# Rows of the seventh image pair moved as three-row pieces, and the last pair's placing steps set closer together

## The chip, the cores and the metric

The kernel runs on one core of a Trainium2 chip. The metric is the time of one execution on the device in microseconds (us), taken as the median of several executions. Five engines work side by side, each through its own queue in a fixed order: TensorE (PE in the profile), VectorE (DVE), ScalarE (ACT), GpSimd (POOL) and SyncE (SP). POOL's and SP's queues also start the DMA transfers. Engines wait for one another through semaphores that are written out in the kernel.

## The reference

Sixteen images of 128 x 512 become 1024 tokens of 64 channels each. One attention block (softmax over keys along the tokens, softmax of queries over the 8 channels of a head) and one mixture of experts follow, each on a layer-normed input and each with a residual.

```python
def _L0_ffn_ref(x, gate_w, gate_b, w1, w2, w3):
    logits = jnp.einsum('bsd,de->bse', x, gate_w) + gate_b
    probs = jax.nn.softmax(logits, axis=-1)
    top_probs, top_idx = jax.lax.top_k(probs, 2)
    top_probs = top_probs / jnp.sum(top_probs, axis=-1, keepdims=True)
    dispatch = jnp.sum(jax.nn.one_hot(top_idx, n_experts, dtype=x.dtype) * top_probs[..., None], axis=-2)
    h1 = jnp.einsum('bsd,edh->bseh', x, w1)
    h2 = jnp.einsum('bsd,edh->bseh', x, w2)
    hidden = jax.nn.silu(h1) * h2
    expert_out = jnp.einsum('bseh,eho->bseo', hidden, w3)
    return jnp.einsum('bseo,bse->bso', expert_out, dispatch)
h = _L0_tok_ref(x, L0_tok_W, L0_tok_b, L0_tok_pos_embed)
h = h + _L0_attn_ref(_layernorm(h, axis=-1), ...)
h = h + _L0_ffn_ref(_layernorm(h, axis=-1), ...)
```

Only the two chosen experts of a token count, so the kernel computes only these.

## The kernel before

The 16 images go in 8 pairs, counted 0 to 7 here as in the code; the seventh pair is pair 6, the last one pair 7. A pair has 2048 tokens, as 16 columns of 128.

*Front part of a pair.* Embedding, attention, the second layer norm and the gate's logits run in about twenty steps; `Plan` says in which step or half step of a pair each operation stands, `BEGUN` at which step of the program a pair begins (pair 6 at 65, pair 7 at 78). Then every token is placed: `pick` finds its two experts, the rank matmuls count how many rows come before it for the same expert, and `find_places` turns that into row numbers in a table sorted by expert. The table lies in DRAM (`rows_scratch`).

*Moving the rows.* For pairs 0 to 6, POOL scatters the rows to the table by 32 indirect DMAs (line 674): per column one for the first expert, one for the second, 128 rows of 512 bytes each. Pair 7 is in `PIECED`: there a column's 256 rows are first sorted on the chip. VectorE builds a 0/1 matrix, the route (lines 1257 and 1262), TensorE multiplies the rows by it (line 1538, three matmuls a column), ScalarE copies the result out (line 842), and POOL writes it with one indirect DMA of 96 pieces of three rows (line 661), so 16 instead of 32. Tiles of such a pair have 126 rows in place of 128, and it has 13 groups of four tiles where the others have 12.

*Back part.* The table is read back by SP in groups of four tiles, one group per step. In step s TensorE does, in this order: the input products of group g = s - 23 (`project_in`), the transposes of the hidden units of g - 1 (`turn_hidden`, bank `hidT_ps`), the operations of the pairs that stand at s, the transposes of the rows of g + 2 (`turn`, bank `turn_ps`, line 1571), the output products of g - 2 (`project_out`, line 1614), and the operations that stand at s + 0.5. ScalarE copies the banks out and forms tanh, VectorE multiplies. SP stores the outputs to DRAM (`y_scratch`).

*Collecting.* POOL gathers a pair's outputs back to its tokens by 32 indirect DMAs (line 691); `GATHER` names the step at which they begin. `SUMS` names the steps in which ScalarE weighs a quarter of them (line 860) and VectorE adds the second half and the residual (line 1317). Pair 7 is gathered in 16 pieces (line 703) and summed by TensorE through gated routes (lines 1548 and 1562) at the very end.

*What sets the order.* All of this is written out step by step. On POOL the loop over the steps issues, in each step, first the pieces, then the scatters, then the gathers that the tables put there. An engine whose next instruction waits holds all that stands behind it. SP's load of a pair's first group waits until all its scatters have landed, and the stores behind it wait with it.

Of the kernel before, what the change touches and what calls it, by code (L numbers as in the profile page):

```python
# [34 lines left out]
PIECED = (7,)  # L35
# [25 lines left out]
    qturn mixed attend added squares2 ssq2 normed2 zturn zparts logits pick rank odds count base tiles bases2 ends owner""")  # L61
# [3 lines left out]
             rank=15, odds=15, count=15, base=15.5, tiles=None, bases2=None, ends=15.5, owner=16)  # L65
# [3 lines left out]
             rank=16, odds=15.5, count=16.5, base=17, tiles=None, bases2=None, ends=17.5, owner=18)  # L69
# [4 lines left out]
         LATER, LATER, LATER, LATER, LATER._replace(tiles=17.5, bases2=18, ends=18.5, owner=19))  # L74
# [72 lines left out]
def vit_kernel(nc, x, tok_w, tok_b, pos, wk, bk, wq, bq, wv, bv, wr, br, gate_w, gate_b, w1, w2, w3, out):  # L147
# [4 lines left out]
    with ExitStack() as ctx:  # L152
# [6 lines left out]
        def sem(name):  # L159
# [129 lines left out]
        piece_at = sb("piece_at", [P, COLS], U32)  # L289
# [20 lines left out]
                x_cols0[:, :, :].rearrange("p j c -> p (j c)"), squares[:, :])  # L310
        pieces = [place[:, n * one:(n + 1) * one] for place, count in zip(flat, (10, 2, 2, 2)) for n in range(count)]
        assert len(pieces) == COLS and one == PIECE * P
# [47 lines left out]
        pieces_out = sem("pieces_out")  # L360
# [24 lines left out]
        def routes_at(half):  # L385

            for m in PIECED:
                for j in range(COLS):
                    if ROUTES[m] + j // 2 == half:
                        yield m, j  # L390
# [152 lines left out]
        def _(pool):  # L543
# [178 lines left out]
            for s in range(SPAN):  # L722
# [7 lines left out]
                for m, j in gathers_at(s):  # L730
                    if m in PIECED:
# [5 lines left out]
        def _(act):  # L737
# [97 lines left out]
            def take_piece(m, j):  # L835
                wait(act, "piece_ps_ready", j + 1)
                if j == 0:
                    wait(act, "emb_ps_ready", 2 * PAIRS)
                    wait(act, "mean_ps_ready", PAIRS)
                    wait(act, "x_turned", PAIRS)  # L840
                    wait(act, "logits_ps_ready", PAIRS)
                sc.activation(pieces[j][0:PIECES, :], piece_place(j)[0:PIECES, 0:PIECE * 2 * E], ACT.Copy).then_inc(S["piece_ready"], 1)

            def take_gates(j):
# [3 lines left out]
                sc.activation(pieces[j][0:PIECES, :], piece_place(j)[0:PIECES, 0:PIECE * P], ACT.Copy).then_inc(S["gates_turned"], 1)  # L848
# [21 lines left out]
            for s in range(SPAN):  # L870
# [13 lines left out]
                for m, j in routes_at(2 * s - 1):  # L884
                    take_piece(m, j)
# [7 lines left out]
                for m, q in sums_at(s):  # L893
                    if m not in PIECED:
# [3 lines left out]
        def _(dve):  # L898
# [117 lines left out]
            def attend(m, k):  # L1016
# [184 lines left out]

            def find_places(m):
# [466 lines left out]
```

## Time and profile before

| | us |
|---|---|
| median of 3 runs | 754.61 |
| the three runs | 757.6, 754.61, 754.32 |
| profiled execution | 757.5 |
| its span, first to last instruction | 755.7 |
| PE busy | 622.1 (82%) |
| DVE busy | 476.6 (63%) |
| ACT busy | 353.2 (47%) |
| POOL busy | 503.5 (67%) |
| mean granted TensorE clock | 0.877 of full speed |

The span is what the trace covers; 1.8 us of the execution lie around it. Busy shares are means over stages with different limits, so the rows below are taken stage by stage. POOL's busy time counts an indirect DMA from when it is taken up to when its descriptors are written; the pause of 0.30 us before the next one is not counted. "L674" is line 674 of the kernel before.

### The profile page before, as it was taken

What the parts mean: (1) busy time and instruction counts of PE and PEld (TensorE: products, weight loads), DVE (VectorE), ACT (ScalarE), POOL (GpSimd) and SP (SyncE); (2) the same over time, 40 slices, a digit from 0 to 9 for tenths busy, and PEclk for the clock granted to TensorE, in tenths of its full rate; (3) what the DMA queues carried; (4) which work ended last, traced back from release to release, by engine and by line L of the source; (5) the groups of instructions that cost most, each with busy time, mean ns of one, the idle gap of its engine ahead of it and who ended that gap; (6) DMA issues with size and microseconds to landing.
All of it is one profiled execution on the core that took longest, in us unless ns stands there. A gap on an engine that the chain in (4) does not pass through costs nothing.

```text
span 755.7 us, 13960 instructions
## 1 busy us (share of the span) xinstructions
PE 622.1 (82%) x4059; PEld 519.8 (69%) x4059; DVE 476.6 (63%) x1322; ACT 353.2 (47%) x774; POOL 503.5 (67%) x537
## 2 busy tenths in 40 slices
PE   5886687788979998999889998998894888799328
PEld 3365454666568967886779687967884787798228
DVE  5654645567556677767666756766585687598410
ACT  2121311226355647564656456545562557486400
POOL 4362044757577477777777777777777777777773
PEclk9958778589989999999999989998998789898755
DMA  3499504134184329542844284537351635664322
GB/s 82 90 175 345 203 29 111 49 108 120 56 226 132 95 55 230 136 131 65 208 134 131 62 204 120 135 82 165 92 149 57 164 98 158 175 150 98 68 59 59
DMA packets 169200, 94.52 MB, mean 125 GB/s; under 512 B 99551, under 2 KB 153207, under 8 KB 169129
## 3 DMA queue, kind: packets, MB, share of 16 engines
q1 hardware_dynamic: 152728, 67.65, 34.5%
q0 software_dynamic: 15616, 25.59, 12.8%
q8 instruction: 38, 0.62, 0.4%
q10 hardware_dynamic: 784, 0.39, 0.2%
q14 instruction: 34, 0.27, 0.1%
HBM read 45.40 MB, written 48.18 MB: 124 GB/s over the span
## 4 chain that ended last, share of the span: by engine, by line
PE 51%; DVE 20%; issue 9%; POOL 7%; DMA 6%; ACT 5%; ACTq 0%; SPq 0%; POOLq 0%; DVEq 0%
PE h_ps L1593 8%; PE wide_ps L1381 7%; PE y_ps L1614 5%; PE hidT_ps L1606 4%; PE turn_ps L1571 3%; PE wide_ps L1401 3%; DMA hx<-xi_scratch 2%; PE wide_ps L1504 2%; DVE twice_y L1298 2%; POOL rows_scratch L674 2%; POOL kexp L691 2%; POOL hx L691 2%; DMA xi_scratch<-xi 2%; PE wide_ps L1387 2%; ACT sums L860 2%
## 5 line engine op out<-in xcount | busy, mean ns | idle before, releaser
L674 POOL DMA_INDIRECT rows_scratch<-z_parts,place x224 | 224.5, 1002 | 126.9 <-issue 64.9
L691 POOL DMA_INDIRECT sums<-y_scratch,place x192 | 185.1, 964 | 66.2 <-issue 56.4
L1593 PE MATMUL h_ps<-w_hi,rowsT 128*128 (+1 forms) x388 | 117.8, 330 | 15.8 <-DVE hid_all L1300 15.4
L1298 DVE SCALAR_TENSOR_TENSOR twice_y<-tanh,h_ps 128x256 f32<-128x256 f32 (+1 forms) x194 | 80.4, 414 | 52.5 <-ACT tanh L818 31.2
L1593 PE MATMUL h_ps<-w_lo,rowsT 128*128 (+1 forms) x388 | 105.6, 298 | 0.0
L1614 PE MATMUL y_ps<-w_sb,hidT_all 128*128 (+1 forms) x776 | 103.1, 279 | 1.4 <-ACT twice_y L833 1.4
L1614 PEld LDWEIGHTS y_ps<-w_sb,hidT_all 128*128 128x128 f32 (+1 forms) x776 | 100.2, 202 | 2.3 <-issue 2.3
L1593 PEld LDWEIGHTS h_ps<-w_hi,rowsT 128*128 128x128 f32 (+1 forms) x388 | 78.8, 203 | 25.9 <-issue 22.3
L818 ACT ACTIVATE tanh<-h_ps 128x256 f32<-128x256 f32 (+1 forms) x194 | 69.6, 386 | 46.5 <-PE h_ps L1593 42.6
L1300 DVE SCALAR_TENSOR_TENSOR hid_all<-twice_y,h_ps 128x256 f32<-128x256 f32 (+1 forms) x194 | 81.6, 421 | 6.7
L1571 PE MATMUL turn_ps<-ident,rows_all 128*128 128x128 f32 (+1 forms) x388 | 64.4, 292 | 21.0 <-DMA rows_all<-rows_scratch 14.2
L1593 PEld LDWEIGHTS h_ps<-w_lo,rowsT 128*128 128x128 f32 (+1 forms) x388 | 79.7, 206 | 0.3
L807 ACT ACTIVATE rowsT<-turn_ps 128x512 fp32r<-128x512 f32 (+1 forms) x97 | 57.7, 594 | 32.4 <-PE turn_ps L1571 32.0
L1606 PE MATMUL hidT_ps<-ident,hid_all 128*128 128x128 f32 (+1 forms) x388 | 66.2, 299 | 6.7 <-issue 3.6
L1571 PEld LDWEIGHTS turn_ps<-ident,rows_all 128*128 128x128 f32 (+1 forms) x388 | 47.9, 150 | 34.3 <-issue 18.4
L827 ACT ACTIVATE hidT_all<-hidT_ps 128x512 f32<-128x512 f32 (+1 forms) x97 | 58.6, 604 | 16.3 <-PE hidT_ps L1606 14.7
L1381 PE MATMUL wide_ps<-w_patch,x_cols 64*128 64x512 f32 x224 | 56.4, 634 | 3.2 <-DVE w_patch L917 3.2
L1606 PEld LDWEIGHTS hidT_ps<-ident,hid_all 128*128 128x128 f32 (+1 forms) x388 | 48.5, 153 | 11.8 <-issue 9.9
L833 ACT ACTIVATE twice_y<-y_ps 128x256 f32<-128x256 f32 (+1 forms) x97 | 37.1, 382 | 30.0 <-DMA y_scratch<-twice_y 20.2
L1381 PEld LDWEIGHTS wide_ps<-w_patch,x_cols 64*128 64x128 f32 x224 | 21.4, 197 | 23.4 <-issue 18.9
L776 ACT ACTIVATE vals<-wide_ps 128x256 f32<-128x256 f32 x28 | 10.7, 383 | 55.3 <-DVE qs L1055 55.3
L1317 DVE SCALAR_TENSOR_TENSOR sums<-sums,gate 128x64 f32<-128x64 f32 x96 | 21.0, 280 | 21.9 <-ACT sums L860 21.9
(350 smaller groups left out, 1107.0 us busy)
## 6 DMA issues: line engine op xcount, KB each, us to landing
rows_all<-rows_scratch SPq DMA_DIRECT2D x84, 256.0 KB
y_scratch<-twice_y SPq DMA_DIRECT2D x84, 128.0 KB
rows_scratch<-tanh SPq DMA_DIRECT2D x3, 3276.0 KB
xi_scratch<-xi SPq DMA_DIRECT2D x16, 256.0 KB
hx<-xi_scratch SPq DMA_DIRECT2D x14, 256.0 KB
rows_scratch<-z_parts,place POOLq DMA_INDIRECT x224
out<-sums SPq DMA_DIRECT2D x56, 64.0 KB
x_in<-in_x SPq DMA_DIRECT2D x26, 128.0 KB
```

Of the source, the lines that this page charges most:

```text
L674: gp.indirect_dma_start(rows_dram[n], bass.IndirectOffsetOnAxis(ap=place[m % RING][:, r, j:j + 1], axis=0), z_parts[m % 2][:, j // 2, j % ...
L691: gp.indirect_dma_start(y_of[r][apart(m)][:, j // 2, j % 2, :], None, y_dram[m % 3][0:GROUPS[m] * GROUP * width(m), :], bass.IndirectOffse ...
L807: sc.activation(rowsT[g % 2][:, 0:GROUP * w], turn_ps[:, 0:GROUP * w], ACT.Copy).then_inc(S["rowsT_ready"], 1)
L818: sc.activation(tanh[0:w, j, :], h_ps[0:w, :].rearrange("p (j n h) -> p j n h", j=GROUP, n=2)[:, j, 0, :], ACT.Tanh, scale=0.5).then_inc(S ...
L827: sc.activation(hidT[g % 2][:, 0:GROUP * w], hidT_ps[:, 0:GROUP * w], ACT.Copy).then_inc(S["hidT_ready"], 1)
L1298: ve.scalar_tensor_tensor(twice[0:w, j, :], tanh[0:w, j, :], 1.0, halves[:, j, 0, :], ALU.add, ALU.mult).then_inc(S["twice_done"], 1)
L1300: ve.scalar_tensor_tensor(hid[g % 2][0:w, j, :], twice[0:w, j, :], 0.5, halves[:, j, 1, :], ALU.mult, ALU.mult).then_inc(S["hid_done"], 1)
L1381: te.matmul(wide_ps[:, b * 512:(b + 1) * 512], x_cols[second(m)][half, j, :], w_patch[half, j, :, :].rearrange("p t e -> p (t e)"), start= ...
L1571: mm = te.transpose(turn_ps[:, j * w:(j + 1) * w], rows[g % 3][0:w, j, :, :].rearrange("p n e -> p (n e)"), ident[0:w, 0:w])
L1593: mm = te.matmul(h_ps[0:w, j * 256:(j + 1) * 256], rowsT[g % 2][:, j * w:(j + 1) * w], w12[:, bass.ds(experts[g][j], 1), :, :].rearrange(" ...
L1606: mm = te.transpose(hidT_ps[:, j * w:(j + 1) * w], hid[g % 2][0:w, j, :], ident[0:w, 0:w])
L1614: mm = te.matmul(y_ps[0:w, j * E:(j + 1) * E], hidT[g % 2][:, j * w:(j + 1) * w], w3_sb[:, bass.ds(e, 1), :].rearrange("h a d -> h (a d)") ...
```

## The change

Pair 6 joins pair 7 in `PIECED`: its rows go as pieces. While pair 7's pieces use the front part's own bank `wide_ps`, which is free by then, pair 6's front part shares the chip with pair 7's, so its pieces take turns in the two banks of the tiles: an even column in `turn_ps`, an odd one in `hidT_ps` (`piece_place`). The waits that keep these uses apart are added to `move_rows`, `turn` and `turn_hidden`; ScalarE's copy of a piece moves ahead of its copy of the hidden units. `ROUTES` gets a start in half steps and a number of columns for each half step: one column for pair 6 from half step 169, two for pair 7 from 191 (196 before). The finding of the moves is a function of its own with a place in the plan. Pair 7's placing operations stand half a step to two and a half steps earlier, its mean and means one and a half and two steps later. The gathers of pair 4 begin at step 86 (91 before), those of pair 5 at 98 (102), of pair 7 at 124 (123), and the sums are shifted with them. Pair 6 has 13 groups, so there are 98 groups in place of 97.

```diff
-PIECED = (7,)
+PIECED = (6, 7)
...
 PLANS = (AT_ONCE._replace(mean=3.5), AT_ONCE._replace(mean=2.5), FIRST,
-         LATER, LATER, LATER, LATER, LATER._replace(tiles=17.5, bases2=18, ends=18.5, owner=19))
+         LATER, LATER, LATER, LATER._replace(tiles=17.5, bases2=18.75, moves=19, ends=19.5, owner=20),
+         LATER._replace(mean=8, means=8.5, rank=15.5, count=15.5, base=16, tiles=16, bases2=16.5, moves=16.5, ends=17, owner=17.5))
...
-ROUTES = (None, None, None, None, None, None, None, 196)
-
-GATES = 105
+ROUTES = {6: (169, 1), 7: (191, 2)}
+
+GATES = 104
...
-SCATTER = (16, 22, 28, 44, 59, 72, 85, None)
-GATHER = (38, 51, 65, 78, 91, 102, 111, 123)
-SUMS = ([[43 + 14 * m + q for q in range(4)] for m in range(5)]
-        + [[112, 113, 114, 115], [121, 122, 122, 123], [124, 125, 126, 127]])
+SCATTER = (16, 22, 28, 44, 59, 72, None, None)
+GATHER = (38, 51, 65, 78, 86, 98, 111, 124)
+SUMS = ([[43 + 14 * m + q for q in range(4)] for m in range(4)]
+        + [[94, 95, 96, 97], [107, 108, 109, 110], [122, 123, 123, 124], [125, 126, 127, 128]])
...
-        def piece_place(j):
-
-            return wide_ps[:, j % 2 * 512:(j % 2 + 1) * 512]
+        def in_between(m):
+
+            return m < PAIRS - 1
+
+        def piece_place(m, j):
+
+            return (turn_ps, hidT_ps)[j % 2][:, :] if in_between(m) else wide_ps[:, j % 2 * 512:(j % 2 + 1) * 512]
...
                 if 0 <= g < GROUPS_ALL:
                     activate(g)
+                for m, j in routes_at(2 * s - 1):
+                    take_piece(m, j)
                 if 0 <= g - 1 < GROUPS_ALL:
                     copy_hidT(g - 1)
                 if 0 <= s - GATES - 2 < COLS:
                     take_gates(s - GATES - 2)
-                for m, j in routes_at(2 * s - 1):
-                    take_piece(m, j)
...
+            def find_moves(m):
+
+                i = nth(m)
+                wait(dve, "base_ps_ready", m + 1)
...
-            def move_rows(m, j):
-
+            def move_rows(m, j, g):
+
+                i = COLS * nth(m) + j
                 if j == 0:
                     wait(pe, "z_split", m + 1)
-                    wait(pe, "piece_at_ready", 1)
-                wait(pe, "route_ready", j + 1)
-                wait(pe, "piece_ready", j - 1)
+                    wait(pe, "piece_at_ready", nth(m) + 1)
+                if in_between(m):
+
+                    wait(pe, *(("rowsT_ready", g + 2), ("hidT_ready", g))[j % 2])
+                wait(pe, "route_ready", i + 1)
+                wait(pe, "piece_ready", i - 1)
...
                 wait(pe, "rowsT_ready", g)
+                wait_pieces(2 * (g - 2 + LAG) - 1)
...
                 wait(pe, "hidT_ready", g)
+                wait_pieces(2 * (g + LAG))
+                if g + LAG == step_of(PIECED[0], 18):
+                    wait(pe, "moves_ready", 2)
...
                 if 0 <= g < GROUPS_ALL:
                     project_in(g)
+                for m, j in routes_at(2 * s - 1):
+                    move_rows(m, j, g)
                 if 0 <= g - 1 < GROUPS_ALL:
                     turn_hidden(g - 1)
                 for m, k in steps_at(s):
                     attend(m, k)
-                for m, j in routes_at(2 * s - 1):
-                    move_rows(m, j)
```

POOL's queue from the end of pair 3's gathers on. Before, one pair's launches stand together: pair 6's scatters, pair 4's gathers, pair 7's pieces, pair 5's gathers.

```order
L674 DMA rows_scratch<-z_parts,place 6552x128 x32
L691 DMA sums<-y_scratch,place 128x64 x32
L661 DMA rows_scratch<-w_patch,piece_at 3744x384 x10
L661 DMA rows_scratch<-x_in,piece_at 3744x384 x2
L661 DMA rows_scratch<-x_cols,piece_at 3744x384 x2
L661 DMA rows_scratch<-squares,piece_at 3744x384 x2
L691 DMA sums<-y_scratch,place 128x64 x32
```

Now, from the same place (L667 are pieces, L697 gathers; pair 6's pieces end with the two from `base`, pair 7's begin with the ten from `w_patch`):

```order
L667 DMA rows_scratch<-w_patch,piece_at 3744x384 x4
L697 DMA sums<-y_scratch,place 128x64 x4
L667 DMA rows_scratch<-w_patch,piece_at 3744x384 x2
...
L667 DMA rows_scratch<-base,piece_at 3744x384 x2
L697 DMA sums<-y_scratch,place 128x64 x4
L667 DMA rows_scratch<-w_patch,piece_at 3744x384 x10
L667 DMA rows_scratch<-x_in,piece_at 3744x384 x2
L697 DMA sums<-y_scratch,place 128x64 x4
L667 DMA rows_scratch<-x_cols,piece_at 3744x384 x2
L667 DMA rows_scratch<-squares,piece_at 3744x384 x2
L697 DMA sums<-y_scratch,place 128x64 x28
```

Pair 6's 16 pieces have 28 of pair 4's gathers between them, in runs of 4, 4, 6, 4, 6 and 4, and the remaining 4 behind; 4 of pair 5's gathers stand among pair 7's pieces.

TensorE in step 86, from the input products on to the transposes of the next rows; before (the third query of pair 7 is L1398 and L1401):

```order
L1577 TENSOR_LOAD owner [waits owner_ready]
L1606 MATMUL hidT_ps<-ident,hid_all 128x128 [waits hidT_ready,hid_done]
L1606 MATMUL hidT_ps<-ident,hid_all 128x128 x3
L1398 MATMUL wide_ps<-qv_bias,ones_r 128x512 [waits q_shifted,v_ready]
L1401 MATMUL wide_ps<-proj_qv,hx 128x256 x2
L1571 MATMUL turn_ps<-ident,rows_all 128x128 [waits rowsT_ready,rows_in2]
L1571 MATMUL turn_ps<-ident,rows_all 128x128 x3
```

The same place now (L1570 is a piece of pair 6, L1523 pair 7's mean):

```order
L1616 TENSOR_LOAD owner [waits owner_ready]
L1570 MATMUL turn_ps<-z_parts,route 96x128 [waits piece_ready,route_ready,rowsT_ready]
L1570 MATMUL turn_ps<-z_parts,route 96x128 x2
L1648 MATMUL hidT_ps<-ident,hid_all 128x128 [waits piece_ready,hidT_ready,hid_done]
L1648 MATMUL hidT_ps<-ident,hid_all 128x128 x3
L1422 MATMUL wide_ps<-qv_bias,ones_r 128x512 [waits q_shifted,v_ready]
L1425 MATMUL wide_ps<-proj_qv,hx 128x256 x2
L1523 MATMUL side_ps<-w_mean,x_cols 128x16 [waits owner_ready]
L1523 MATMUL side_ps<-w_mean,x_cols 128x16 x7
L1610 MATMUL turn_ps<-ident,rows_all 128x128 [waits piece_ready,rowsT_ready,rows_in2]
L1610 MATMUL turn_ps<-ident,rows_all 128x128 x3
```

The wait for `rowsT_ready`, which stood behind the hidden units and the query, now stands ahead of them, and the turn also waits for the copy of the piece.

TensorE around the turn of pair 6's first group, now (L1610 is that turn, L1538 the count of pair 7's rows, which before stood one step later):

```order
L1610 MATMUL turn_ps<-ident,rows_all 128x126 [waits rowsT_ready,rows_in0]
L1610 MATMUL turn_ps<-ident,rows_all 128x126 x3
L1656 ISA [waits y_ready,hidT_ready]
...
L1538 MATMUL side_ps<-ones_b,hot_b 128x1 [waits hot_ready]
L1538 MATMUL side_ps<-ones_b,hot_b 128x1
```

The count has moved up to half a step behind the turn, and not ahead of it.

## Rows read from the trace of the kernel before

**Rows 1.** The page: busy tenths in 40 slices of the span, POOL.

```profile
POOL 4362044757577477777777777777777777777773
```

**Rows 2.** Windows of POOL: start:end, us, busy us (count), PE clock, DMA share, GB/s.

```profile
540.35:582.77 42.42, 32.67 (x32) 0.93 0.38 103
623.15:643.43 20.28, 15.40 (x17) 0.92 0.58 160
685.24:725.52 40.28, 30.52 (x32) 0.76 0.33 70
```

**Rows 3.** Timelines of POOL and PE: start, us, what [idle before <-releaser].

```profile
581.51 0.96 POOL L674 DMA_INDIRECT rows_scratch<-z_parts,place  x1 [0.30 <-issue]
586.54 1.11 PE L1571 MATMUL turn_ps<-ident,rows_all 128*128 128x128 f32 x4 [10.49 <-DMA rows_all<-rows_scratch]
```

**Rows 4.** Timelines of POOL and PE, pair 7's last piece and first group.

```profile
642.21 0.91 POOL L661 DMA_INDIRECT rows_scratch<-squares,piece_at  x1 [0.30 <-issue]
647.87 0.67 PE L1571 MATMUL turn_ps<-ident,rows_all 126*128 126x126 f32 x4 [3.76 <-DMA rows_all<-rows_scratch]
```

**Rows 5.** Timelines of PE, ACT and DVE around step 86.

```profile
529.59 1.91 PE L1495 MATMUL side_ps<-w_mean,x_cols 128*128 128x16 f32 x16
537.29 0.60 PE L1606 MATMUL hidT_ps<-ident,hid_all 128*128 128x128 f32 x4
539.79 0.63 PE L1571 MATMUL turn_ps<-ident,rows_all 128*128 128x128 f32 x4 [0.80 <-ACT rowsT L807]
...
539.07 0.58 ACT L807 ACTIVATE rowsT<-turn_ps 128x512 fp32r<-128x512 f32 x1
544.00 1.05 ACT L779 ACTIVATE qs<-qs 128x1024 f32<-128x1024 f32 x1
...
539.20 0.87 DVE L1317 SCALAR_TENSOR_TENSOR sums<-sums,gate 128x64 f32<-128x64 f32 x4 [1.77 <-ACT sums L860]
```

**Rows 6.** Pair 7's placing: timelines of PE and DVE, and a group of the page.

```profile
588.06 1.97 PE L1614 MATMUL y_ps<-w_sb,hidT_all 128*128 x8 [0.41 <-ACT twice_y L833]
595.98 0.20 PE L1464 MATMUL side_ps<-counted_all,same_expert_b 128*16 128x1 bf16 x2
...
593.09 0.15 DVE L1167 TENSOR_SCALAR thirds<-side_ps 128x2 f32<-128x2 f32 x1
593.79 0.53 DVE L1175 TENSOR_SCALAR counted_all<-ones,counted 128x128 bf16<-128x128 f32 x2
597.76 0.29 DVE L1193 TENSOR_SCALAR tiles_all<-ones,tiles 16x128 bf16<-16x128 f32 x1
601.14 0.75 DVE L1211 TENSOR_TENSOR placed<-hot,side_ps 128x256 f32<-128x256 f32 x2
605.24 0.16 DVE L1223 TENSOR_SCALAR place<-slots_u 128x32 uint32<-128x32 uint32 x1
...
L1300 DVE SCALAR_TENSOR_TENSOR hid_all<-twice_y,h_ps 128x256 f32<-128x256 f32 (+1 forms) x194 | 81.6, 421 | 6.7
```

**Rows 7.** Timelines of PE, DVE and ACT: pair 7's pieces, the first and last two.

```profile
611.19 0.71 PE L1538 MATMUL wide_ps<-z_parts,route 128*96 128x128 f32 x6
...
632.87 1.26 PE L1538 MATMUL wide_ps<-z_parts,route 128*96 128x128 f32 x6
...
622.00 0.65 DVE L1257 TENSOR_SCALAR route<-slot_id,slots_f 128x288 fp32r<-128x288 f32 x2
622.56 0.94 DVE L1262 SCALAR_TENSOR_TENSOR route<-slot_id,slots_f,route 128x288 fp32r<-128x288 f32 x2
...
623.63 0.92 ACT L842 ACTIVATE w_patch<-wide_ps 96x384 f32<-96x384 f32 x2 [2.00 <-PE wide_ps L1538]
```

**Rows 8.** Timelines of PE and ACT: output products, and pair 5's last quarter weighed.

```profile
657.74 1.00 PE L1614 MATMUL y_ps<-w_sb,hidT_all 128*128 x8
672.59 0.99 PE L1614 MATMUL y_ps<-w_sb,hidT_all 128*126 x8
704.82 1.09 PE L1614 MATMUL y_ps<-w_sb,hidT_all 128*126 x8 [0.39 <-ACT twice_y L833]
...
686.85 1.44 ACT L860 ACTIVATE sums<-sums,mean_all,gate 128x64 f32<-128x64 f32 x4 [1.15 <-DMA sums<-y_scratch,place]
```

More of the change, by code:

```diff
@@ L60 @@
 Plan = namedtuple("Plan", """embed squares normed bases mean means keys kmax kexp kturn queries values qexp qsum context scales mix
-    qturn mixed attend added squares2 ssq2 normed2 zturn zparts logits pick rank odds count base tiles bases2 ends owner""")
+    qturn mixed attend added squares2 ssq2 normed2 zturn zparts logits pick rank odds count base tiles bases2 moves ends owner""")
 FIRST = Plan(embed=(0.75, 1, 1.5, 2), squares=2.5, normed=2.5, bases=3.5, mean=5.5, means=5.5, keys=4.5, kmax=4.5, kexp=5, kturn=5,
@@ L64 @@
              attend=10, added=10.5, squares2=10.5, ssq2=11, normed2=11.5, zturn=12.5, zparts=12.5, logits=13, pick=13.5,
-             rank=15, odds=15, count=15, base=15.5, tiles=None, bases2=None, ends=15.5, owner=16)
+             rank=15, odds=15, count=15, base=15.5, tiles=None, bases2=None, moves=None, ends=15.5, owner=16)
 LATER = Plan(embed=(1, 1.5, 2, 2), squares=2.5, normed=2.5, bases=3.5, mean=6.5, means=6.5, keys=5, kmax=5.5, kexp=6, kturn=6,
@@ L68 @@
              attend=11, added=11.5, squares2=11.5, ssq2=12, normed2=12.5, zturn=13.5, zparts=13.5, logits=14, pick=14.5,
[L69 removed]
+             rank=16, odds=15.5, count=16.5, base=17, tiles=None, bases2=None, moves=None, ends=17.5, owner=18)
 AT_ONCE = FIRST._replace(zturn=12, logits=12.5, pick=12.5, rank=13, count=13, odds=14.5, base=13.5, ends=13.5, owner=14)
 PLANS = (AT_ONCE._replace(mean=3.5), AT_ONCE._replace(mean=2.5), FIRST,
[L74 removed]
+         LATER, LATER, LATER, LATER._replace(tiles=17.5, bases2=18.75, moves=19, ends=19.5, owner=20),
+         LATER._replace(mean=8, means=8.5, rank=15.5, count=15.5, base=16, tiles=16, bases2=16.5, moves=16.5, ends=17, owner=17.5))
 XI_OUT, HX_IN, X_NEXT = 2, 3, 4
@@ L288, in vit_kernel @@
         moves = placed[0]
-        piece_at = sb("piece_at", [P, COLS], U32)
+        piece_at = [sb(f"piece_at{n}", [P, COLS], U32) for n in range(2)]
         piece_from = sb("piece_from", [P, COLS], U32)
@@ L309, in vit_kernel @@
         flat = (w_patch[:, :, :, :].rearrange("p j t e -> p (j t e)"), x_in0[:, :, :].rearrange("p r f -> p (r f)"),
-                x_cols0[:, :, :].rearrange("p j c -> p (j c)"), squares[:, :])
-        pieces = [place[:, n * one:(n + 1) * one] for place, count in zip(flat, (10, 2, 2, 2)) for n in range(count)]
-        assert len(pieces) == COLS and one == PIECE * P
+                x_cols0[:, :, :].rearrange("p j c -> p (j c)"))
+        pieces = [[place[:, n * one:(n + 1) * one] for place, count in zip(flat + (last,), (10, 2, 2, 2)) for n in range(count)]
+                  for last in (base0[:, :, :, :].rearrange("p t b e -> p (t b e)"), squares[:, :])]
+        assert len(pieces[0]) == COLS and one == PIECE * P
         x_in = (x_in0[:, :, :], twice_y[:, :].rearrange("p (r f) -> p r f", r=2))
@@ L359, in vit_kernel @@
         scattered = [sem(f"scattered{n}") for n in range(3)]
-        pieces_out = sem("pieces_out")
+        pieces_out = [sem(f"pieces_out{n}") for n in range(len(PIECED))]
         rows_in = [sem(f"rows_in{n}") for n in range(3)]
@@ L1112, in attend @@
                     count_tiles(m)
+                if k == plan.moves:
+                    find_moves(m)
                 if k == plan.ends:
```

95 lines of the change are left out of this document (57 added, 38 removed).

## The prediction

> **What bounds the kernel now.** I read the slices of the page first: POOL's row stands at 7 in every slice from the fifteenth, about 265 us, to the last but one [rows 1]. That is no engine with a quarter of its time free. The windows of three stretches of POOL show 32 launches in 42.42 us, 16 in 20.28 and 32 in 40.28 [rows 2]: one indirect DMA each 1.26 to 1.33 us, of which about 0.95 is counted busy, with the next one close behind. (The x17 counts a neighbour at the edge.) So from about 265 us POOL is a queue that never empties, and the order of the launches in it is fixed. The end is POOL too: after the last gathers of pair 6 at 725.52 come the 16 of pair 7 and the closing sums, 755.7 - 725.52 = 30.2 us.
>
> Then I read where TensorE waits for this queue. The scatter of pair 6 ends late: its last launch starts at 581.51 and TensorE, idle for 10.49 us, turns the pair's first tile group at 586.54 [rows 3]. For pair 7, which already goes as pieces, the last launch starts at 642.21 and its first group is turned at 647.87, 5.66 us later [rows 4]. Taking launches out of the queue before 581 therefore looks like pure gain. The question is whether POOL still has something to launch.
>
> **The change, part by part.** I follow three hinges: T, the turn of pair 6's first group (586.54 before); X, the end of POOL's gathers of pair 5 (685.24); and the end (755.7).
>
> *POOL's saving.* 32 scatters of rows (42.42 us) become 16 of pieces (20.28 us): 22.1 us less in the queue [rows 2]. One piece costs 20.28/16 = 1.27 us, one gather 40.28/32 = 1.26.
>
> *Its new order, up to T.* Before, all 32 scatters stood together. Now 28 of the 32 gathers of pair 4 stand between the pieces (first order fence). POOL is free for pair 6 at 540.35 as before, since nothing ahead of it changes. The sixteenth piece starts at 540.35 + 15 x 1.27 + 28 x 1.26 = 594.7, if POOL never waits; with the 5.66 us of rows 4, T = 600.3. So the interleaving alone makes T 13.8 us later, though POOL has then done most of pair 4's gathers, which before came after 582.77.
>
> *What the pieces add in TensorE's steps.* Four pieces stand at the head of that queue without a gather between them, so the fourth is wanted at 540.35 + 3 x 1.27 = 544.2. It comes at the end of the step in which pair 7's third and fourth queries are formed. ScalarE can copy it only behind the exponential of the queries, which before ran from 544.00 to 545.05 [rows 5]; with half of 0.92 for the copy [rows 7] that is 545.5, a wait of 1.3 us at the least, and T = 601.6. The step also grows. The piece in the turn bank needs the copy out of that bank, the one TensorE waited for until 539.79; the transposes and the query, which ran before that wait (537.29 to 539.79 less the wait of 0.80, 1.70 us), now stand behind it (second order fence), and so does pair 7's mean, moved there from a step and a half earlier (1.91 us). To this come the product (half of 0.90), two pieces' routes on VectorE (622.00 to 623.50, 1.50) and two copies (0.92) [rows 5, 7]. Together 6.5 us: the fourth piece at 552.0, a wait of 7.8, T = 608.1. VectorE's own gap of 1.77 us at 539.20 [rows 5] can hold the routes, so I take T = 608.1 - 1.8 = 606.3, and keep 601.6 and 608.1 for the range. The other pieces come in time: after each pair stand four or six gathers, 5 to 7.6 us, about a step. Routes, copies and products of the later steps lie beside these gathers; without that cover each step would add some 3 us.
>
> *A rule on VectorE beside POOL.* The 16 piece launches of pair 7 took 1.27 us each with route operations running beside many of them, no more than gathers at 1.26 [rows 2, 7], so I add nothing for the 32 new route operations. The Trainium skill ("SBUF — State Buffer", "Who interferes with whom") says that a VectorE copy or tensor-scalar in a two-port mode locks GpSimd out for the whole instruction. By that rule the 16 first route operations of 0.33 us would delay as many launches, 5.3 us, and the time would be 765.2; the 1.27 of the trace includes such operations already and speaks against it, and I leave it 3 chances in 100 inside the slowest case below.
>
> *The last pair's small operations.* They move up by up to five half steps: count, base, tiles, moves and places now follow within two steps. But its count matmuls stand behind the turn at T in TensorE's order, so none runs during the stall; the chain starts there. From T: the output products end at 588.06 + 1.97 - 586.54 = 3.5; count 1.2 (593.09 to 594.32); base and tiles 2.1 (595.98 to 598.05); one tile multiply of four operations at 0.42, 1.7; moves and places 4.3 (601.14 to 605.40); one sum of pair 4 on VectorE 1.3 (0.87 and a longer 0.42, estimate); another multiply 1.7; routes 1.5; product and copy 0.9 [rows 5 to 7]. That is 18.2, and six hand-overs between engines at an estimate of 0.2 (539.07 + 0.58 to 539.79 shows 0.14) make 19.4. Before, the first two pieces were ready after 611.19 - 586.54 = 24.7 on TensorE, but POOL was not there until 623.15.
>
> *From T to X.* Two pieces follow every (632.87 - 611.19)/7 = 3.10 us [rows 7], so pieces eleven and twelve are ready at T + 19.4 + 5 x 3.10 = T + 34.9. Behind them POOL has these two, 4 gathers, 4 pieces and 28 gathers: 6 x 1.27 + 32 x 1.26 = 47.9. X = T + 82.8 = 689.1, 3.9 us later than before. POOL meanwhile idles: after the last piece of pair 6 (at T - 4.7, its launch over) only four gathers are left, until T + 0.3; the first piece of pair 7 comes at T + 19.4. These 19 us, with the waits before T, eat the 22.1.
>
> *From X to the end.* POOL gathers pair 6 until X + 40.3. TensorE is held too: ScalarE weighs the last quarter of pair 5 in step 110 (115 before) and stands there until the gather lands. Before, it began that at 686.85, X + 1.6, and the last output product came 17.97 us and six steps later, at 704.82. Now twelve steps follow, six more at (672.59 - 657.74)/5 = 2.97 [rows 8]; the thirteenth tile group of pair 6 is one of them. Product at X + 1.6 + 18.0 + 17.8 = X + 37.4; its 1.1, the copy and the store to DRAM are an estimate of 4.3, half of rows 4's two DMAs and 1.5 for the rest. So pair 7's outputs lie there at X + 41.7 and POOL waits 1.4 us. End: X + 41.7 + 30.2 = X + 71.9 = 761.0.
>
> *At nothing:* the removed rank matmuls of pair 6, its count and moves (they lie in steps in which POOL is behind anyway); pair 7's old stall of 3.76 us [rows 4], which goes, since its pieces now end some six steps ahead of their turn, but TensorE then waits in step 110 instead; the longer descriptors, in the 1.27.
>
> *Sum.* 761.0 against the span of 755.7: +5.3. The profiled execution took 757.5 in all, so it would take 762.8. The median of the three runs is 754.61, below the profiled one; the difference put on it gives 759.9 us, and the rivals below stand on the median too.
>
> **Rivals.** *The queue stays full:* if pair 7's pieces are ready when pair 4's gathers end, all 22.1 us come back: 732.5. For it: rows 2. Against it: the chain of 19.4 us behind T has only 5 us of gathers as cover. *A shorter chain:* T at its low end (-4.7), the sum and one multiply beside TensorE's work (-3.0), hand-overs free (-1.2), no wait at the end (-1.4), 10.3 in all: 749.6. The gap of 1.77 speaks for it; that each step names the other engine's last result, against. *No change:* only T at its low end, 755.2. For it: TensorE and ScalarE also idle in places within those steps; against it: the second order fence, which puts a chain of waits where there was slack. *TensorE becomes the bound of pair 6's pieces:* the shared banks chain TensorE to ScalarE's copies, and each of the eight steps costs 1.50 + 0.92 + 0.45 = 2.9 more, and once the 3.6 of rows 5. TensorE reached the stalled turn at 586.54 - 10.49 = 576.05; it would get there at 602.9, the last piece launched there, T = 608.6 and the time 762.2; were pair 7's pieces, on the same chain, paced at an estimate of 4.0 instead of 3.10, it would be 5 x 0.9 more, 766.7. It decides from about 25 us of added work on (from 576.05 to the 600.9 at which the last launch stands at T = 606.3); below that POOL's queue hides it.
>
> **How the numbers follow.** This measurement can tell 0.5% from no change, 3.8 us: faster is under 750.8, slower over 758.4. Forecast 0.39 (own range 756 to 764, a quarter of it under 758.4), no change 0.27, shorter chain 0.14, full queue 0.08, TensorE as bound 0.12. Faster 0.14 + 0.08 = 0.22; same 0.27 + 0.10 = 0.37; slower 0.29 + 0.12 = 0.41. The range leaves out the full queue and the far end of the last case: 747 to 767.
>
> **What would show it.** Right: the pieces of pair 6 on POOL with a gap of 1 to 8 us before the fourth; the stalled turn near 606; about 20 us in which POOL launches nothing, from then on; no stall before pair 7's first group; ScalarE waiting in step 110 for a gather. Wrong: POOL without a gap from 540 to the end, or a turn before 598, or pair 7's first piece within 14 us of it.

## The result, and the profile after

The changed kernel takes 765.89 us (median of four, 762.46 to 774.62), the kernel before 754.54 beside it. The ratios in this document leave out runs in a slower state, here the 774.62, and compare the means of the others: 764.75 to 755.25, ratio 1.0126, 95% interval 1.0079 to 1.0172. A second series ("changed again" in the table of experiments) gave 767.65 against 755.38, 1.0148 (1.0098 to 1.0197). So the change costs 9.5 to 11.2 us. Forecast were 759.9 and a range of 747 to 767; the second median lies just outside it.

| profiled execution | before | after |
|---|---|---|
| execution, span | 757.5, 755.7 | 765.45, 763.7 |
| PE, DVE, ACT busy | 622.1, 476.6, 353.2 | 633.5, 490.9, 362.5 |
| POOL busy | 503.5 | 489.5 |

The page's slices of the changed kernel show where POOL runs dry; before, every digit from the fifteenth to the last but one was 7 [rows 1]:

```profile
POOL 4353047767574777777777777777377616777773
```

The 3 that breaks the long run of 7s is the slice from 534.6 to 553.7 us, the 6 and the 1 that follow it the slices from 592 to 630. POOL's windows from its first launch for pair 6 (P from here on) to the first gather of pair 7, before and then after (us, busy us with the count of instructions, PE clock, DMA share, GB/s):

```profile
540.35:725.52 185.17, 141.26 (x144) 0.85 0.48 120
```

```profile
533.99:733.46 199.47, 125.58 (x128) 0.86 0.45 115
```

Sixteen launches fewer, 14.3 us more. POOL's timeline after (start, us, instruction, idle before and its releaser) has the reason: pair 6's first four pieces, its last piece and the last of the four gathers behind it, pair 7's first piece:

```profile
533.99 0.94 POOL L667 DMA_INDIRECT rows_scratch<-w_patch,piece_at  x1 [0.30 <-PE turn_ps L1610]
538.50 0.93 POOL L667 DMA_INDIRECT rows_scratch<-w_patch,piece_at  x1 [3.57 <-ACT w_patch L853]
541.97 0.91 POOL L667 DMA_INDIRECT rows_scratch<-w_patch,piece_at  x1 [2.54 <-ACT w_patch L853]
549.21 0.91 POOL L667 DMA_INDIRECT rows_scratch<-w_patch,piece_at  x1 [6.33 <-ACT w_patch L853]
...
601.17 0.93 POOL L667 DMA_INDIRECT rows_scratch<-base,piece_at  x1 [0.30 <-issue]
...
606.19 0.94 POOL L697 DMA_INDIRECT sums<-y_scratch,place  x1 [0.30 <-issue]
626.28 0.93 POOL L667 DMA_INDIRECT rows_scratch<-w_patch,piece_at  x1 [19.15 <-ACT w_patch L853]
629.61 0.91 POOL L667 DMA_INDIRECT rows_scratch<-w_patch,piece_at  x1 [1.16 <-ACT w_patch L853]
...
692.55 0.94 POOL L697 DMA_INDIRECT hx<-y_scratch,place  x1 [0.30 <-issue]
...
733.46 0.93 POOL L709 DMA_INDIRECT sums<-y_scratch,piece_from  x1 [0.30 <-issue]
```

A pause of 0.30 belongs to every launch. What goes beyond it adds up to 11.54 us ahead of the second, third and fourth pieces, 18.85 ahead of pair 7's first and 4.52 among pair 7's pieces (the 1.16 is the first of five): 34.91. The rest, 199.47 - 34.91 = 164.56, is 1.286 us for each of 128 launches, and 185.17/144 is 1.286 too. So the change saved 20.6 us of launches and lost 34.9 in waits.

The turn T that pair 6's first group waits for, and the chain behind it to pair 7's first piece (timelines of PE, DVE and ACT; [rows 3, 6, 7] are the same operations before):

```profile
606.46 1.10 PE L1610 MATMUL turn_ps<-ident,rows_all 126*128 126x126 f32 x4 [9.38 <-DMA rows_all<-rows_scratch]
609.45 0.24 PE L1538 MATMUL side_ps<-ones_b,hot_b 128*128 128x1 bf16 x2
612.39 0.20 PE L1488 MATMUL side_ps<-counted_all,same_expert_b 128*16 128x1 bf16 x2
614.93 0.59 PE L1504 MATMUL wide_ps<-to_piece,counted_all 128*96 128x512 bf16 x2
624.26 1.15 PE L1570 MATMUL wide_ps<-z_parts,route 128*96 128x128 f32 x6
...
617.35 0.86 DVE L1341 SCALAR_TENSOR_TENSOR sums<-sums,gate 128x64 f32<-128x64 f32 x4
622.86 0.64 DVE L1281 TENSOR_SCALAR route<-slot_id,slots_f 128x288 fp32r<-128x288 f32 x2
...
693.62 1.43 ACT L871 ACTIVATE sums<-sums,mean_all,gate 128x64 f32<-128x64 f32 x4 [6.43 <-DMA sums<-y_scratch,place]
```

The count (609.45) stands behind the turn, the tile work and one sum of pair 4 (617.35) stand between, and the first product comes at T + 17.8. The last row is ScalarE's wait in step 110.

The two traces don't begin alike. TensorE's windows of 110 to 165 us, long before the change acts, before and after:

```profile
110.00:165.00 55.00, 42.68 (x197) 0.75 0.30 85
```

```profile
110.00:165.00 55.00, 41.88 (x231) 0.81 0.33 95
```

The profiled execution of before was granted a lower clock in this stretch and reached P 6.4 us later (540.35 against 533.99). This stretch alone does not settle P: "thinner again" below had 0.75 in it too, and its P was 534.17. But over the fourteen profiles P goes with the mean granted clock of the first 265 us: 533.99 to 534.88 in the five with 0.88, 539.16 to 540.35 in the three with 0.85 (one of them with pieces for pair 6). So the experiments are compared by distances from P, and the times by their ratios.

### The profile page after: what moved, and what is told of

Its sections match the earlier page's. It is cut to its first block, busy times and chain, and to the rows that moved or that the text cites. A ratio compares the mean times of both kernels' runs of the same rounds, so it can differ in the third digit from the quotient of the medians.

```text
span 763.7 us, 14233 instructions
## 1 busy us (share of the span) xinstructions
PE 633.5 (83%) x4126; PEld 529.6 (69%) x4126; DVE 490.9 (64%) x1369; ACT 362.5 (47%) x795; POOL 489.5 (64%) x521
## 3 DMA queue, kind: packets, MB, share of 16 engines
q1 hardware_dynamic: 153524, 67.96, 34.9%
## 4 chain that ended last, share of the span: by engine, by line
PE 51%; DVE 20%; issue 10%; POOL 8%; ACT 5%; DMA 5%; ACTq 0%; DVEq 0%; POOLq 0%
PE h_ps L1632 8%; PE wide_ps L1405 7%; PE y_ps L1656 6%; POOL sums L697 5%; PE hidT_ps L1648 4%; PE turn_ps L1610 3%; PE wide_ps L1425 3%; PE wide_ps L1532 2%; DVE twice_y L1322 2%; DMA hx<-xi_scratch 2%; PE wide_ps L1411 2%; POOL rows_scratch L667 2%; DMA xi_scratch<-xi 1%; ACT sums L871 1%; PE h_ps L1600 1%
## 5 line engine op out<-in xcount | busy, mean ns | idle before, releaser
L680 POOL DMA_INDIRECT rows_scratch<-z_parts,place x192 | 192.0, 1000 | 107.8 <-issue 56.4
L697 POOL DMA_INDIRECT sums<-y_scratch,place x192 | 186.9, 973 | 66.2 <-issue 55.8
L1656 PE MATMUL y_ps<-w_sb,hidT_all 128*128 (+1 forms) x784 | 106.8, 283 | 0.8 <-ACT twice_y L839 0.7
L1656 PEld LDWEIGHTS y_ps<-w_sb,hidT_all 128*128 128x128 f32 (+1 forms) x784 | 104.1, 207 | 1.4 <-issue 1.4
L1610 PE MATMUL turn_ps<-ident,rows_all 128*128 128x128 f32 (+1 forms) x392 | 65.7, 294 | 20.7 <-ACT rowsT L813 11.0
L1610 PEld LDWEIGHTS turn_ps<-ident,rows_all 128*128 128x128 f32 (+1 forms) x392 | 49.5, 153 | 34.2 <-issue 23.7
L813 ACT ACTIVATE rowsT<-turn_ps 128x512 fp32r<-128x512 f32 (+1 forms) x98 | 57.9, 591 | 26.3 <-PE turn_ps L1610 26.3
L1648 PEld LDWEIGHTS hidT_ps<-ident,hid_all 128*128 128x128 f32 (+1 forms) x392 | 48.9, 154 | 12.6 <-issue 11.7
L667 POOL DMA_INDIRECT rows_scratch<-w_patch,piece_at x20 | 19.5, 976 | 40.8 <-ACT w_patch L853 37.1
L871 ACT ACTIVATE sums<-sums,mean_all,gate 128x64 f32<-128x64 f32 x96 | 34.2, 430 | 9.1 <-DMA sums<-y_scratch,place 9.1
```

The lines of the kernel that those rows point to most:

```text
L680: gp.indirect_dma_start(rows_dram[n], bass.IndirectOffsetOnAxis(ap=place[m % RING][:, r, j:j + 1], axis=0), z_parts[m % 2][:, j // 2, j % ...
L697: gp.indirect_dma_start(y_of[r][apart(m)][:, j // 2, j % 2, :], None, y_dram[m % 3][0:GROUPS[m] * GROUP * width(m), :], bass.IndirectOffse ...
L813: sc.activation(rowsT[g % 2][:, 0:GROUP * w], turn_ps[:, 0:GROUP * w], ACT.Copy).then_inc(S["rowsT_ready"], 1)
L1610: mm = te.transpose(turn_ps[:, j * w:(j + 1) * w], rows[g % 3][0:w, j, :, :].rearrange("p n e -> p (n e)"), ident[0:w, 0:w])
L1648: mm = te.transpose(hidT_ps[:, j * w:(j + 1) * w], hid[g % 2][0:w, j, :], ident[0:w, 0:w])
L1656: mm = te.matmul(y_ps[0:w, j * E:(j + 1) * E], hidT[g % 2][:, j * w:(j + 1) * w], w3_sb[:, bass.ds(e, 1), :].rearrange("h a d -> h (a d)") ...
```

## The experiments

The theory is the forecast's: POOL's queue sets T, and the placing chain behind T sets pair 7's first piece. The rival: TensorE's and ScalarE's longer steps set both. All distances in us; "pauses" is POOL's idle time beyond 0.30 a launch from P to pair 7's gathers. Distances come from one profile a kernel, and T - P differed by 0.4 us between two profiles of the changed kernel and by 3.3 between two of the thinner one.

| kernel | T - P | first piece - T | pauses | end - P | ratio to before (95%) |
|---|---|---|---|---|---|
| before | 46.2 | 36.6 | 0 | 215.4 | |
| changed | 72.5 | 19.8 | 34.9 | 229.7 | 1.0126 (1.0079 to 1.0172) |
| changed again | 72.8 | 19.7 | 34.9 | 229.1 | 1.0148 (1.0098 to 1.0197) |
| gathers later | 71.4 | 19.3 | 33.1 | 228.2 | 1.0151 (1.0094 to 1.0208) |
| thinner | 71.8 | 20.0 | 35.7 | 229.7 | 1.0120 (1.0084 to 1.0156) |
| thinner again | 68.5 | 19.2 | 31.8 | 225.0 | one run, 760.95 us |
| pieces alone | 74.2 | 19.1 | 57.9 | 251.2 | one run, 790.66 us |
| weighing moved | 68.5 | 19.9 | 31.0 | 225.0 | 1.0120 (1.0053 to 1.0188) |
| placing earlier | 71.6 | 17.0 | 33.5 | 227.4 | 1.0176 (1.0115 to 1.0237) |
| old placing | 73.4 | 28.1 | 46.3 | 241.4 | 1.0318 (1.0242 to 1.0394) |
| placing alone | 46.3 | 26.6 | 0 | 215.9 | 1.0017 (0.9987 to 1.0046) |
| weighing moved, before | 45.5 | 36.6 | 0 | 214.4 | 0.9986 (0.9966 to 1.0006) |
| combined | 60.7 | 16.3 | 20.0 | 215.0 | 1.0000 (0.9965 to 1.0036) |
| combined, sums later | 60.3 | 16.3 | 17.4 | 212.1 | 0.9935 (0.9907 to 0.9964) |

One sum covers the whole table: end - P less the pauses is 193.2 to 195.1 in every kernel with pieces for pair 6, and 214.4 to 215.9 where it goes as rows. The time from P is POOL's launches, its pauses and the closing 30 us. The sum doesn't say what makes the pauses; that is what the edits below are for.

**The gathers begun one step later.**

```diff
-GATHER = (38, 51, 65, 78, 86, 98, 111, 124)
+GATHER = (38, 51, 65, 78, 87, 98, 111, 124)
```

> Changed kernel with the gathers of pair 4 begun one step later (87 for 86), so that 24 instead of 28 of them stand ahead of pair 6's last piece. Theory (GpSimd's queue sets T, the turn of pair 6's first group): the last piece's product was at 593.88 and its launch only at 601.17; with 4 to 6 launches fewer ahead of it, it goes at about 595.5 to 596, T = 600.7 to 601.5 instead of 606.46, pair 7's first piece about 20 us later at 621, the span about 758.5, ratio to before 1.006. Rival (TensorE's lengthened steps set T): T stays at 606, span 764, ratio 1.0126.

T came 1.1 us earlier behind P, not 5 to 6. POOL's first six launches for pair 6 show why:

```profile
540.25 1.20 POOL L667 DMA_INDIRECT rows_scratch<-w_patch,piece_at  x1 [0.31 <-issue]
541.75 0.93 POOL L667 DMA_INDIRECT rows_scratch<-w_patch,piece_at  x1 [0.30 <-issue]
544.14 0.91 POOL L667 DMA_INDIRECT rows_scratch<-w_patch,piece_at  x1 [1.47 <-ACT w_patch L853]
553.02 0.91 POOL L667 DMA_INDIRECT rows_scratch<-w_patch,piece_at  x1 [7.97 <-ACT w_patch L853]
556.50 0.91 POOL L667 DMA_INDIRECT rows_scratch<-w_patch,piece_at  x1 [2.57 <-ACT w_patch L853]
560.31 1.77 POOL L667 DMA_INDIRECT rows_scratch<-w_patch,piece_at  x1 [2.90 <-ACT w_patch L853]
```

The four gathers that left had been cover: pieces five and six now wait 2.57 and 2.90, about as long as four launches take. The theory's size fell, since I took gathers out where the pieces weren't ready; the rival was not shown by it.

**The gathers thinned out late, not early**, and once more for a second profile:

```diff
-    if GATHER[m] + (... (COLS + j * GROUPS_NEXT) // (2 * COLS)) == s:
+    if ((86, 87, 88, 89, 90, 91, 92, 93)[j // 2] if m == 4 else GATHER[m] + (...)) == s:
```

> Changed kernel with 4 launches of pair 4's gathers in each step from 86 to 93 (before 4 or 6), so that 24 and not 28 stand ahead of pair 6's last piece, the first ones where they stood. Distances from the first piece launch of pair 6 (533.99 in the changed kernel), since the traces begin up to 6 us apart. Theory (behind the fourth piece GpSimd's queue sets T): T falls by four launches, 5.0, from 72.5 to 67.5 us after the first piece; pair 7's first piece 5 us earlier with it, span about 759, ratio 1.006. Rival (TensorE's and ScalarE's steps set T): T stays at 72.5, ratio 1.0126.

> The kernel with thinner gathers once more, for a second profile. In the first one TensorE's granted clock was 0.68 from 534 to 550 us (0.96 in the changed kernel's), and the fourth piece came 4.7 us later beside the first. Theory (queue and TensorE's steps bind T together, the clock decides which): with a clock above 0.9 in these windows T is 67 to 69 us behind the first launch. Rival (the thinner gathers do nothing): 72.

The first profile missed (71.8), the second met the expectation (68.5, at a granted clock of 1.00 from 534 to 550). In the first, TensorE was granted the lower level (1.2 of 2.4 GHz) for 541 to 547, where the changed kernel had full clock. TensorE's windows, first profile and changed kernel:

```profile
535.00:541.00 6.00, 3.67 (x20) 0.82 0.29 75
541.00:547.00 6.00, 6.00 (x28) 0.50 0.21 60
```

```profile
535.00:541.00 6.00, 3.67 (x26) 0.97 0.28 88
541.00:547.00 6.00, 6.00 (x48) 1.00 0.33 90
```

It was busy 3.67 of the 6 us ahead of it in both, so these rows do not say why it fell in one. It cost the fourth piece a wait of 11.02 for 6.33. That is the 4.7 us of the expectation; the piece itself came 2.2 us later behind P (17.5 for 15.2), since the second piece had come sooner. In the second profile pair 6's last two pieces and T read:

```profile
593.44 0.93 POOL L667 DMA_INDIRECT rows_scratch<-base,piece_at  x1 [0.30 <-issue]
596.78 1.14 POOL L667 DMA_INDIRECT rows_scratch<-base,piece_at  x1 [2.41 <-ACT base L853]
...
602.71 1.10 PE L1610 MATMUL turn_ps<-ident,rows_all 126*128 126x126 f32 x4 [4.06 <-DMA rows_all<-rows_scratch]
```

Now the last piece waits for its copy. Four launches fewer, and TensorE's and ScalarE's pace sets T. In the time (1.0120) the gain is too small to tell.

**The pieces alone**, all gathers of pair 4 behind them:

```diff
-GATHER = (38, 51, 65, 78, 86, 98, 111, 124)
+GATHER = (38, 51, 65, 78, 93, 98, 111, 124)
...
-        + [[94, 95, 96, 97], ...
+        + [[97, 98, 99, 100], ...
```

> Changed kernel with all gathers of pair 4 put behind pair 6's last piece (begun at step 93; sums of pair 4 at 97 to 100). GpSimd then launches pair 6's pieces as they come. Theory: T falls to what TensorE's and ScalarE's steps allow, last product at 593.88 in the changed kernel, so about 66 us after the first piece launch instead of 72.5, and the launches show waits of several us between most pieces; the 28 gathers come later, so the span is about 15 us longer, near 780. Rival (TensorE's steps already set T in the changed kernel): T stays at 72 or more behind the first piece.

POOL waits before 15 of the 16 pieces, 49 us in all, and T is 74.2 behind P: later than in the changed kernel. The theory's 66 failed, and the rival's sign came true. But the granted clock was 0.71 from 534 to 550 (0.96 in the changed kernel), so this is TensorE's and ScalarE's pace at a low clock. In the changed kernel POOL launched without a pause from the fourth piece to the last, whose product was there at 593.88, 7.3 us ahead of its launch; there the queue set that part of T. My estimate from these runs and thinner again: at a good clock the steps of TensorE and ScalarE allow about 68, at a bad one 74, and POOL's queue, its first waits included, wants 72.5. So the two lie close together; no run has the pieces alone at a full clock.

**ScalarE's weighing moved.** The changed kernel's third piece waited on a chain of ScalarE (timelines of ACT and PE): the weighing of pair 3's sums stands ahead of the copy out of the turn bank, and the piece goes into that bank.

```profile
538.11 1.42 ACT L871 ACTIVATE sums<-sums,mean_all,gate 128x64 f32<-128x64 f32 x4
539.44 0.58 ACT L813 ACTIVATE rowsT<-turn_ps 128x512 fp32r<-128x512 f32 x1
...
540.07 0.47 PE L1570 MATMUL turn_ps<-z_parts,route 128*96 128x128 f32 x3 [2.33 <-ACT rowsT L813]
```

```diff
                 if 0 <= g - 1 < GROUPS_ALL:
                     copy_hidT(g - 1)
+                for m, q in sums_at(s):
+                    if m == 3:
+                        weigh(m, q)
...
-                    if m < PAIRS - 1:
+                    if m < PAIRS - 1 and m != 3:
                         weigh(m, q)
```

> Changed kernel with one edit: ScalarE weighs pair 3's quarters (steps 85 to 88, 1.42 us each) behind its copy of the hidden units, no longer at the end of the step, where the copy out of the turn bank and with it the next piece wait behind it. All 28 gathers stay between the pieces. Theory as forecast (GpSimd's queue sets T): the first four pieces come some 3 us earlier, two steps of 1.4, and T with them, about 69 to 70 us behind the first launch instead of 72.5. Rival (TensorE and ScalarE set T): all four steps count, T falls by 5.7, to 67 behind the first launch. If pieces and queue bind together, the fall is that of the slower of the two, 3 or less, and the span near 761, ratio 1.008.

```profile
534.88 0.94 POOL L667 DMA_INDIRECT rows_scratch<-w_patch,piece_at  x1 [0.30 <-issue]
536.26 0.96 POOL L667 DMA_INDIRECT rows_scratch<-w_patch,piece_at  x1 [0.44 <-ACT w_patch L853]
538.45 0.90 POOL L667 DMA_INDIRECT rows_scratch<-w_patch,piece_at  x1 [1.23 <-ACT w_patch L853]
545.65 0.91 POOL L667 DMA_INDIRECT rows_scratch<-w_patch,piece_at  x1 [6.30 <-ACT w_patch L853]
...
603.38 1.10 PE L1613 MATMUL turn_ps<-ident,rows_all 126*128 126x126 f32 x4 [12.44 <-DMA rows_all<-rows_scratch]
```

T is 68.5 behind P, 4.0 less, between the two expectations, but not all of this is the weighing. It made the third piece's wait 1.23 for 2.54, which was 2.54 or 2.55 in seven of the eight other profiles with pieces for pair 6 and the weighing in its old place. The larger part, 3.57 to 0.44 before the second piece, is not shown to be the edit's: that piece's copy stands ahead of the weighing in the changed kernel, and its wait lay between 0.30 and 3.58 in those eight. TensorE reached the stalled turn 7.0 us sooner behind P (603.38 - 12.44 - 534.88 = 56.1, before 606.46 - 9.38 - 533.99 = 63.1), but its stall grew from 9.38 to 12.44: here POOL's queue sets T. So the weighing cost 1.3 us at the third piece, and this is a cost of the pieces' place in the turn bank that the forecast did not have. In the time (1.0120) nothing can be told from it. The same edit in the kernel before:

> Kernel before with the same edit on ScalarE (pair 3's quarters weighed behind the copy of the hidden units). Theory: pair 6 goes as rows there, GpSimd's queue is full, and nothing of it waits for ScalarE's copy; time as before, ratio 0.997 to 1.003. Rival (the place of the weighing costs by itself): 2 to 5 us faster, ratio 0.994 to 0.997.

0.9986: no gain there, as the theory had it.

**The placing of pair 7**: half a step earlier still, back at the places of before, and moved without the pieces of pair 6.

```diff
-LATER._replace(mean=8, means=8.5, rank=15.5, count=15.5, base=16, tiles=16, bases2=16.5, moves=16.5, ends=17, owner=17.5))
+LATER._replace(mean=8, means=8.5, rank=15, count=15, base=15.5, tiles=15.5, bases2=16, moves=16, ends=16.5, owner=17))
...
-ROUTES = {6: (169, 1), 7: (191, 2)}
+ROUTES = {6: (169, 1), 7: (189, 2)}
```

> Changed kernel with all placing operations of pair 7 half a step earlier still (rank and count at 15, ahead of the stalled turn; base and tiles 15.5, bases2 and moves 16, ends 16.5, owner 17, routes from half step 189). Theory (POOL's 19 us without a launch are the placing chain of pair 7 that starts at T): the count is done during the stall, the chain from T shrinks from 19.8 to about 16 us, T stays at 606.5, the span falls by about 4 to 760, ratio 1.008. Rival (the backlog of tile work after the stall on TensorE and VectorE sets the first piece, not the chain): the first piece stays at T + 19 to 20, span 764, ratio 1.0126.

The count ran in the stall (matmul at 596.29, T at 605.64), and the first piece came at T + 17.0 instead of 19.8. The mechanism held, with 2.8 of the 3.8 us expected. The time did not fall (1.0176): it scatters too widely to show 2.8 us, and 2.3 more were lost among the pieces.

```diff
-LATER._replace(mean=8, means=8.5, rank=15.5, ..., owner=17.5))
+LATER._replace(mean=8, means=8.5, tiles=17.5, bases2=18, moves=18.5, ends=18.5, owner=19))
...
-ROUTES = {6: (169, 1), 7: (191, 2)}
+ROUTES = {6: (169, 1), 7: (196, 2)}
...
-GATES = 104
+GATES = 105
```

> Changed kernel with pair 7's placing operations back at the places of before (rank 16 to owner 19, routes from half step 196); its mean and means stay where the change put them. Theory: GpSimd is free after T but the first piece comes at T + 24.7 or later (the distance of before), 5 to 9 us later than in the changed kernel; span 769 to 773, ratio 1.019 to 1.025. Rival (the places in the plan do not matter, the tile work does): span 764, ratio 1.0126.

```profile
635.74 0.93 POOL L667 DMA_INDIRECT rows_scratch<-w_patch,piece_at  x1 [27.75 <-ACT w_patch L853]
```

The first piece comes at T + 28.1, the pauses grow by 11.4 and end - P by 11.7. So beside pair 6's pieces the closer placing is worth 11.7 us, more than the 5 to 9 expected; without it the change would have cost over 3%.

> Kernel before with only the closer placing operations of pair 7 (and its routes from half step 191, its mean later); pair 6 still goes as rows. Theory: GpSimd has scatters and gathers to launch until about 623 whatever the placing does, so the pieces are ready early and wait for it; time as before, ratio 0.997 to 1.003, the stall of 3.8 us before pair 7's first group remains. Rival (closer operations cost by themselves, on TensorE and VectorE): 3 to 5 us slower, ratio 1.004 to 1.007.

With pair 6 as rows it is worth nothing (1.0017): POOL launches without a pause. Only the stall before pair 7's first group, which the theory had left as it was, fell from 3.76 to 1.21 [rows 4], off POOL's path.

**Combined**, four edits: gathers of pair 4 in fours at steps 85 to 90, 92 and 93, the weighing moved, the placing earlier, sums of pair 5 later; then also the sums of pair 4 out of the chain and the gathers of pair 5 from step 99 (97 in the first). The tables of the second, against the changed kernel:

```diff
-GATHER = (38, 51, 65, 78, 86, 98, 111, 124)
+GATHER = (38, 51, 65, 78, 86, 99, 111, 124)
-        + [[94, 95, 96, 97], [107, 108, 109, 110], ...
+        + [[98, 99, 100, 101], [111, 112, 113, 114], ...
```

> Changed kernel with four edits: gathers of pair 4 in fours at steps 85 to 90, 92 and 93; placing of pair 7 half a step earlier, as in the run with the placing earlier (and gathers of pair 5 from 97); ScalarE weighs pair 3's quarters behind the copy of the hidden units and not at the end of the step, ahead of the copy out of the turn bank; sums of pair 5 at steps 111 to 114. Theory: pieces of pair 6 come 1.4 us earlier in each of four steps, T is 60 to 63 us behind the first piece, the first piece of pair 7 17 us behind T, span 748 to 752, ratio 0.99 to 0.997. Rival (TensorE's steps set T): T at 66 or later, span 755, ratio 1.000 to 1.003.

> As the combined kernel, but the sums of pair 4 at steps 98 to 101 instead of 94 to 97 and the gathers of pair 5 from 99, so that neither ScalarE's weighing (1.43 us a step) nor VectorE's sum (1.3) stands in the placing chain of pair 7. Theory: first piece of pair 7 about 14 us behind T instead of 17, span 745 to 750, ratio 0.985 to 0.993. Rival (these operations lie beside the chain): first piece at T + 17, as the combined kernel.

The first met its distances (60.7 and 16.3), but its ratio was 1.0000, as the rival had it. The pauses fall to 20.0 and 17.4, less than the 20.6 saved, and the second is a little faster than the kernel before: median 750.11 against 754.05, ratio 0.9935 (0.9907 to 0.9964). Its first piece did not come sooner than in the first (T + 16.3 in both), so that part of the expectation failed; the gain is in the pieces behind it: all 16 launched in 21.4 us for 28.8, partly since four gathers stand among them in the first.

## Why the prediction was right, and where its sizes were off

Direction and mechanism were right: slower, because POOL, its 16 launches saved, waits for pieces. The size was not: 5.3 us were forecast, 9.5 to 11.2 measured. From P the profile took 9.0 us more than forecast (229.7 for 220.7): 6.5 up to T, 3.3 from T to X, less 0.8 behind X. That its span still came within 2.7 us (763.7 for 761.0) is luck, since P lay 6.4 us earlier. By its own steps:

- *POOL's saving*: 22.1 forecast, 20.6 measured. The mean launch is 1.286 both ways, but the dearer scatters are gone from it: pieces took 1.26 us (1.27 before), all 96 gathers 1.29 (1.27 before, and 1.26 in the 32 that the forecast took). The gathers' 1.9 us together are about what is missing. The Trainium skill ("SBUF — State Buffer", "Who interferes with whom") lets a VectorE instruction in a two-port mode hold GpSimd off. 32 route operations more did not show in the pieces' launches, and the gathers' 1.9 us, whose cause is open, are less than the 5.3 of that rule, so the trace speaks against that price here; whether these operations ran in such a mode no run shows.
- *The wait before the fourth piece* is the term that was mis-sized: one wait of 6.0 us (1.3 to 7.8) forecast, three measured: 3.27, 2.24 and 6.03, 11.54 together. I reckoned that pieces two and three would be there when POOL was. They come one in a half step like the others, and the one in the turn bank also waits for the weighing, 1.3 us, which I had left out. Behind the fourth the pieces came in time, as forecast.
- *T* came at 606.46, forecast 606.3. That they meet is chance: P was taken at 540.35, as before, and was 533.99. From P, T was forecast 66.0 and measured 72.5: 5.5 for the waits, 1.4 for the launches behind them (51.96 for 50.5), less 0.4.
- *The chain from T to pair 7's first piece*: 19.4 forecast, 19.8 measured, 19.1 to 20.0 in seven profiles wherever T was. That the count stands behind the stalled turn was shown by moving it.
- *From there to X*: piece eleven was launched at 643.37, so two pieces took (643.37 - 626.28)/5 = 3.42 us, not 3.10; the 38 launches from there took 49.2, not 47.9; X = T + 86.1 for 82.8.
- *X to the end*: 71.15 for 71.9. ScalarE waited in step 110 (693.62, X + 1.07) as forecast. Pair 7's outputs were in time: POOL did not wait before 733.46, where I had 1.4.
- *TensorE as the bound* was given 0.12 and a limit of 25 us of added work. Between the product of step 84 and the stalled turn the changed kernel took 24.8 more: 597.08 - 524.97 against 576.05 - 528.75. The two products (PE), before and after:

```profile
528.75 1.00 PE L1614 MATMUL y_ps<-w_sb,hidT_all 128*128 x8
```

```profile
524.97 1.00 PE L1656 MATMUL y_ps<-w_sb,hidT_all 128*128 x8
```

  So it came near its limit. It was at the turn 4.1 us before the last piece was launched (597.08 and 601.17), and four launches fewer were enough for that piece to wait for its copy in thinner again.
- *The full queue* and *the shorter chain* fell. *No change* fell as well: both intervals lie above 1.005.

Open: from P, the profiles differ by 14 us, the times by 9.5 to 11.2. P lay 2.5 us earlier on average in the eleven profiles with pieces for pair 6 (536.0) than in the three without (538.5). Within both kinds it went with the clock of the first 265 us, where the change does not act; that the clocks fell so by chance was not tested.

## What to carry to other kernels

Work taken out of a full queue is only won if what comes next in that queue is ready: sum the pauses of the bounding queue, and compare them with the launches saved. Launches put between pieces are cover as long as the pieces come slower than the queue, and a delay as soon as they come faster, so look for the pace of both. When one engine's copy frees a bank for another use, everything that stands ahead of that copy becomes part of the new chain.

## What the runs showed of the hardware

An indirect DMA cost POOL 1.27 to 1.29 us on average over the 128 or 144 launches from P on, in all fourteen profiles, though a piece launch moves 96 pieces of 1536 bytes, a scatter 128 rows of 512 and a gather 128 rows of 256; before, the three kinds took 1.27, 1.33 and 1.26 [rows 2]. The same kernel's P lay at 533.99 and 539.01 in two executions, with a mean granted TensorE clock of 0.88 and 0.86 in the first 265 us, and 4.4 of these 5.0 us were still there at the end (spans of 763.7 and 768.1). From the copy of pair 6's third piece to that of the fourth it took 7.7 us in the eight profiles that were granted 0.93 to 1.00 from 541 to 547 us and 9.4 to 12.6 in the three that were granted 0.50 to 0.72 there.
